# Front attention, 64 heads: a loop over four heads written out head by head

## The reference

```python
q = split_heads(x @ Wq + bq); k = split_heads(x @ Wk + bk); v = split_heads(x @ Wv + bv)
scores = einsum('bhid,bhjd->bhij', q, k)
rel = einsum('bhid,pd->bhip', q, rel_key)           # p = 256 positions
bias = take_along_axis(rel, clip(j - i + p - 1, 0, p - 1))
logits = where(j <= i, (scores + bias) * scale, -inf)
out = einsum('bhij,bhjd->bhid', softmax(logits), v)
```

## Time and profile before

| | us |
|---|---|
| median of 3 runs | 4380.38 |
| lowest and highest | 4378.44, 4381.74 |
| the profiled execution, its own time | 4380.54 |
| its span, first to last instruction | 4378.7 |
| front attention in it, about | 106 to 952 |
| loop of front attention, rounds 4 to 63, about | 146 to 911 |

### The profile page before, as it was taken

One profiled execution on the slowest core, in us unless ns is written; L12 is line 12 of the kernel. 1 busy time (PEld: TensorE's weight loads), 2 busy tenths in 40 slices (PEclk: granted clock), 3 DMA queues, 4 the chain that ended last, 5 costly groups with the idle time before them and its releaser, 6 DMA issues. The chain is left out here.

```text
span 4378.7 us, 124836 instructions
## 1 busy us (share of the span) xinstructions
PE 4132.4 (94%) x44000; PEld 2958.4 (68%) x44000; DVE 3601.4 (82%) x8420; ACT 3593.7 (82%) x6842; POOL 2336.7 (53%) x2840
## 2 busy tenths in 40 slices
PE   4799999975999999999999999999999999999993
PEld 2466666653777777777777777777777777777773
DVE  6588888876888888888888888888888888888884
ACT  1799989952888888888888888888888888888882
POOL 1000000005776767676677676767776777667761
PEclk7899999986999999999999999999999999999996
DMA  6777777731111111111111111111111111111111
GB/s 226 220 224 236 230 223 237 224 116 65 46 41 46 36 43 41 46 41 46 33 46 41 46 41 41 38 46 41 46 36 43 41 46 41 42 37 46 41 46 45
DMA packets 258632, 358.17 MB, mean 82 GB/s; under 512 B 44404, under 2 KB 216156, under 8 KB 257884
## 3 DMA queue, kind: packets, MB, share of 16 engines
q1 hardware_dynamic: 258140, 351.55, 26.7%
HBM read 151.19 MB, written 93.34 MB: 56 GB/s over the span
## 5 line engine op out<-in xcount | busy, mean ns | idle before, releaser
L1375 PE MATMUL la_ps<-la_Wqkv,la_xsT 128*128 128x512 f32 x2304 | 1191.1, 612 | 2.9 <-DVE la_rsk L1089 1.6
L1032 POOL TENSOR_TENSOR la_rt<-la_rt,la_rn 128x1024 f32<-128x1024 f32 x384 | 722.9, 1904 | 27.5
L1089 DVE TENSOR_TENSOR la_rsq<-la_ps,la_tab 128x1024 f32<-128x1024 f32 x384 | 469.2, 1222 | 93.5 <-ACT la_sq L1233 91.3
L1096 DVE TENSOR_REDUCE la_ssum<-la_sq 128x8 f32<-128x512 f32 x768 | 502.4, 674 | 0.0
L1410 PEld LDWEIGHTS la_ps<-la_kT,la_qB 128*64 128x64 f32 x12288 | 390.5, 138 | 145.8 <-issue 145.8
L1233 ACT ACTIVATE la_sq<-la_ps 128x512 f32<-128x512 f32 x768 | 448.8, 597 | 43.6 <-PE la_ps L1375 30.2
L1375 PEld LDWEIGHTS la_ps<-la_Wqkv,la_xsT 128*128 128x128 f32 x2304 | 377.4, 190 | 141.3 <-issue 94.0
L1089 DVE TENSOR_TENSOR la_rsk<-la_ps,la_tab 128x1024 f32<-128x1024 f32 x384 | 466.1, 1214 | 6.1 <-ACT la_sq L1233 3.9
L1441 PEld LDWEIGHTS la_ps<-la_Wo,la_oT 128*128 128x128 f32 x3072 | 366.7, 192 | 110.2 <-issue 103.4
L481 POOL COPY at_vh<-V 128x64 f32 (+1 forms) x64 | 15.2, 238 | 786.2 <-PE at_ps L680 785.4
L1410 PE MATMUL la_ps<-la_kT,la_qB 128*64 128x64 f32 x12288 | 433.2, 224 | 0.0
(11 more groups left out here) (168 smaller groups left out, 10204.4 us busy)
## 6 DMA issues: line engine op xcount, KB each, us to landing
at_band<-skew_scratch SPq DMA_DIRECT2D x64, 1536.0 KB, 7.3
la_vs<-la_v SPq DMA_DIRECT2D x192, 384.0 KB, 3.6
skew_scratch<-at_R SPq DMA_DIRECT2D x64, 1024.0 KB, 6.7
la_vs<-la_v SPq DMA_DIRECT2D x192, 128.0 KB, 3.4
la_Wqkv<-in_wqkv SPq DMA_DIRECT2D x28, 384.0 KB, 3.7
kt_scratch<-pr_k SPq DMA_DIRECT2D x24, 384.0 KB, 3.2
qt_scratch<-pr_q SPq DMA_DIRECT2D x24, 384.0 KB, 4.1
at_qh<-qt_scratch SPq DMA_DIRECT2D x64, 144.0 KB
```

The source lines that it names most:

```text
L1032: e.tensor_tensor(heads(rt, w), heads(rt, w), wide(rn[:, w * H:(w + 1) * H], D), ALU.mult)\
L1089: e.tensor_tensor(dst.rearrange("p f (h d) -> p f h d", d=D), ps[:, c % 2, :].rearrange("p (h d) -> p h d", d=D).unsqueeze(1).to_broadcast ...
L1096: e.tensor_reduce(ssum[:, c * 8:(c + 1) * 8], sq[:, c % 2, :].rearrange("p (h d) -> p h d", d=D), AX.X, ALU.add).then_inc(ss_ev.sem, 1)
L1375: e.matmul(ps[:, c % 2, :], xsT[:, m * P:(m + 1) * P], Wqkv[:, ds(layer(n) % 2, 1), c * 512:(c + 1) * 512], start=True, stop=True)\
```

## The change

On each of the five engines the driver of front attention's rounds is replaced; `body`, the order in it, the buffers and the waits are the same. The first four and the last four rounds were written out before as well. All calls in other parts stay.

```diff
--- before.py
+++ after.py
@@ -467,7 +467,7 @@
                 for n, m in t.back(1):
                     skewed(n, m)
                     band_in(n, m)
-            rounds(e, body, HEADS_A, RING_A, DEEPEST_A)
+            straight(e, body, HEADS_A, RING_A, DEEPEST_A)
...
```

## The result

| | before | after |
|---|---|---|
| median of 8 runs each, us | 4381.06 | 4392.48 |
| lowest and highest | 4378.44, 4384.05 | 4387.11, 4396.84 |
| ratio, with its 95% interval | | 1.0026 (1.0017 to 1.0035) |
| the profiled execution, its own time | 4380.54 | 4392.65 |
| its span | 4378.7 | 4390.9 |

The written-out kernel is slower, by 11.4 us in the medians and 12.1 us between the two profiled executions. The forecast was 4374.5 with a range from 4361 to 4388, so the time came out on the other side of the kernel before and above the range.

A forecast was written before the change was run, and what follows sets the result against it. Bound: front attention's ring from band issue through q and k's landing at L644 to VectorE's minimum and the next band issue. 60 times (-0.05 - 0.10 - 0.07 + 0.12) = -6.0 us from 4380.54 gave 4374.5, range 4361 to 4388.

The forecast's parts named there:

- The two rings: Front attention: band issue to L644, minimum, next band issue, 12.65 us, taken as bound; a VectorE chain nearly as long.
- The second ring: Front attention: values(0) through TensorE to the last scores, back through VectorE; written out between 12.24 and 12.44 us, say 12.33.
- Earlier issue of q and k: SP in front attention: q and k issued closer behind the band, gaining 0.05 us a round.
- SP's register operation: SP in front attention: band issue follows VectorE's minimum by 0.02 instead of 0.12 us, gaining 0.10 a round.
- TensorE's wait: TensorE at L644: the load itself carries the wait for q and k, gaining 0.07 us a round, bounds 0 and 0.10.
- The branch: Loop branch in one of four front attention rounds: removal taken as 0, possibly 1.5 us in all.
- Packets of code: Front attention's DMA engines: instruction transfers of written-out code delay q and k, costing 0.12 us a round.
- The sum: Front attention's 60 changed rounds: gains of 0.05, 0.10 and 0.07 against a cost of 0.12, -6.0 us in all.
- The third: Front attention: code packets among q and k's lengthen every round by 0.47 us, less 0.17 gained; 4398.5 us, chance 0.15.
- The first: Front attention: instruction fetches are harmless, gains stay, rounds of 12.45 us; 4366 us, chance 0.24.
- the second rival: Front attention: L644 waits for nothing, VectorE's chain alone is left, rounds of 12.33 us; 4359 us, chance 0.07.
- Layers: Sign in the layers, same code elsewhere in memory: a change over 2 us would make the prediction wrong altogether.

## Why the prediction was wrong

**The two rings: right.** Band issue to L644, on to the minimum and to the next band was the bound, and VectorE's ring stood just behind: with q and k ahead of the band the round goes from 12.69 to 12.60, and no further. The second ring's length in the loop is thus measured at 12.58 to 12.65, and written out at 12.42 to 12.44.

**Earlier issue of q and k (-0.05): nothing.** q is issued 0.41 behind the band in all rounds of the kernel after but one. The 1.20 of the earlier trace rows, and with it the 0.78 to be gained, was read from a round with the loop's branch, one in four; in the three others of the kernel before it is 0.90:

```profile
527.96 0.36 SPq L461 DMA_DIRECT2D at_band<-skew_scratch  x1
528.86 0.83 SPq L448 DMA_DIRECT2D at_qh<-qt_scratch  x1
```

With SP alone written out L644 stands at +8.61, in the undisturbed rounds of the kernel after at +8.51, against +8.57 before; the 0.06 are the load's, which starts 0.07 closer behind the landing. Zero was the lower bound.

**SP's register operation (-0.10): right in place.** The minimum ends at 532.68 and 352.60, the band is issued at 532.72 and 352.62. By itself it brings nothing that the runs tell, since the second ring was 0.1 behind.

**TensorE's wait (-0.07): right at L644, and missed at L680.** L644 follows the landing by 0.04 instead of 0.11. But the loads of values(0) now carry their wait too. Kernel after, VectorE's product, its copy and the loads:

```profile
520.12 0.18 DVE L528 RECIPROCAL at_rc<-at_ps 128x4 f32<-128x4 f32 x1
520.34 0.19 DVE L531 TENSOR_TENSOR X<-at_ps,at_rc 128x32 f32<-128x32 f32 x1
520.44 0.29 DVE L518 COPY at_pT<-at_ps 128x128 f32<-128x128 f32 x1
...
520.94 0.19 PEld L680 LDWEIGHTS at_ps<-at_pT,at_vh 128*32 128x32 f32 x8 [0.24 <-issue]
```

The copy ends at 520.73, the load follows 0.21 later. Before, it began at 515.75 and the load at 516.09: with the same 0.29, 0.05 behind. So VectorE starts its copy 0.32 after the reciprocal's start instead of 0.63, and 0.16 of the 0.31 is given back at the load. Not all of it is the load's own wait: the copy's end to the load takes 0.11 with TensorE alone written out, and 0.11 in most rounds with all but TensorE written out. Each side by itself adds 0.06, both together 0.16; no run shows why VectorE's side adds any. The chain takes 0.82, between 0.97 before and the 0.72 that was forecast from the earlier trace rows; with TensorE left in its loop it takes 0.72 (501.59 to 502.31 there). That fits the shortest second ring, 12.37 against 12.44, which is the one with TensorE left in its loop. Where the first ring binds, this loss costs nothing.

**Local gains together.** Rounds without a packet ahead of L644 went from 12.69 to 12.54: 0.15 of the 0.22 that the sum had. By the four rounds without any packet, 12.44, it would be 0.25, with a price of the packets higher by the same 0.10; only the difference of the two is measured.

**The branch (0): nearly right.** With q and k ahead of the band every fourth round of the loop is 0.07 longer, 1 us in 15 turns, inside the 1.5 that the prediction allowed.

**Packets of code (+0.12): the step that failed.** Their number was right: 42 and 37 in 54 rounds, 0.78 and 0.69 a round, where 0.79 and 0.72 were forecast. Their price was not. From the groups, 18 rounds lose 0.94 each and 22 lose 0.08: (16.9 + 1.8) / 54 = 0.35 a round, three times the term and above its upper bound of 0.29. So the mechanism was in the prediction, and the size of this term turned the sign. The main reason is the price. It was bounded by the one round with a visible loss, 0.47, as if that were the most that a packet can do; the 18 rounds lose twice that on average. Further, queue 8 was priced at 0 to 0.06 from the round whose L644 is at 181.86, taken as typical. The groups say that it wasn't. Queues of that round of the kernel before, whose band is issued at 173.16, in 176.6 to 178.3:

```profile
q1 hardware_dynamic: 421, 0.65, 102.5%
q8 instruction: 1, 0.02, 3.5%
```

and of the round from 132.95, in 138 to 139:

```profile
q1 hardware_dynamic: 245, 0.38, 105.0%
q14 instruction: 1, 0.01, 2.1%
```

The first starts 3.49 behind its band issue, outside the stretch in which packets of queue 8 did harm; the second 5.07 behind, inside that of queue 14. The two rows on which the price hung, 0.12 and 0.47, were one round outside and one inside, and the better reading was a mixture: the share of rounds that are hit, times the price there. Even so, a third of the rounds at 0.47 makes 0.16; it takes the measured 0.94 to reach the loss.

**The sum.** 60 times (0.35 - 0.15) = 12 us, where the profiled executions differ by 12.1 and the stage itself by 10.3; forecast was -6.0. All of the error is the packets' term (0.23 a round, 14 us) and 0.07 a round less local gain (4 us), if the split by the groups is right. By the rule of the Trainium skill that the prediction named (Runtime: NRT & Kernel Launch, section Instruction fetch mechanics) the packets' term is 0; the measurement has 0.35. The trace agrees with the rule as far as TensorE's own supply goes, since no wait of TensorE for "issue" is over 0.8 us in the kernel after, and rounds grow all the same where q and k land late, a price that the term of 0 leaves out.

**The rivals.** The third had the mechanism, packets of code among those of q and k, and was given 0.15. It had it in every round at 0.47, which the groups don't show: a third of the rounds lose 0.94, and the mean of 0.35 is three quarters of what it had. Its time, 4398.5, is 6 us over the measured one. Its other half, a band issue held by the skewed write, is not there (0.03 behind the minimum). The first (rounds of 12.45) and the second (no wait for q and k at L644) have their features in the kernel with q and k ahead of the band, whose rounds take 12.44. That its time is the second rival's 4359 is chance: some 7.5 us of it come from the filling, which no rival had. Layers: 1.3 us longer, under the 2 us that would have meant another cause.

**What stays open.** Why a packet of queue 8 delays q and k in many rounds if it starts 5.0 to 5.45 us behind the band's issue, not in all of them, and not at 3.49 or 5.81; no run varied its time by itself. The traces don't say which of the 16 DMA engines a packet takes, so the engine is a rival to the time that stays untested. That the sign turns with the place of q and k is shown; that the position of single packets is the cause of the long rounds rests on the grouping.

## What to carry to other kernels

Before code is written out, look for a transfer on the critical ring: the fetches are packets on DMA engines that the data need too, and one holds an engine for about a microsecond. Their number can be counted ahead from a stretch that is written out already; that came out right here. Their price can't be had from a round or two: with TensorE alone written out, rounds with a packet in the same stretch took from 12.65 to 14.12. Take the transfer out of the ring first; then writing out paid 12 us here, and without it cost 11.

## What the runs showed of the hardware

- An instruction packet of TensorE's code (queue 8, 16 KB) takes 1.12 us on average on its DMA engine among data (42 of them, 0.93 to 1.44), one of queue 14 (8 KB) 0.42 (37, 0.31 to 0.80).
- A loop body of 4 rounds on TensorE brought no code packets in 700 us; one of 12 rounds brought 51, and at each return to its start a gap of 5.7 to 6.3 us, with rounds of up to 23.9 us.
- A wait carried by TensorE's load itself starts it 0.04 behind a DMA's landing (0.11 through a register). Behind VectorE's copy it is the other way round: 0.11 against 0.05 with VectorE in its loop, 0.21 against 0.11 with VectorE written out. The same rewriting gained at one wait and lost at the other.
- A turn of the loop with its branch took 0.07 us in a ring that nothing else disturbed (rounds of 12.65 among rounds of 12.58).
- An idle of 2.21 us ahead of one load was followed by some 10 us at a granted clock of 0.50; late transfer and drop together cost over 6 us.
- GpSimd's 16 KB transfer into one partition went as 32 packets of 512 B, one row of the weights each.
